# A selective scan with a LoRA feed-forward: VectorE writes the step size into the decays' buffer, and ScalarE's copies go

## The reference

```
h = layernorm(x) * (1 + ca) + sa
xp = h @ x_proj_w.T                      # 32 columns for dt, then B (16), C (16)
dt = softplus(xp[:, :32] @ dt_proj_w.T + dt_proj_b)
dA = exp(dt[..., None] * A);  dBx = dt[..., None] * B[:, None, :] * h[..., None]
state = dA_t * state + dBx_t;  y_t = sum over the 16 states of state * C_t
x = x + ga * (y + D * h)
h = layernorm(x) * (1 + cb) + sb
gate = h @ gate_w.T + (h @ gate_a.T) @ gate_b.T      # up alike, rank 16
hidden = silu(gate) * up                             # 2752 wide
x = x + gb * (hidden @ down_w.T + (hidden @ down_a.T) @ down_b.T)
```

## Time and profile before

| | |
|---|---|
| device time, median of 3 (range) | 2398.21 us (2397.32 to 2401.29) |
| profiled execution, its time | 2402.57 us |
| profiled execution, its span | 2400.6 us |
| TensorE busy | 2085.1 us (87%) |
| VectorE, ScalarE, GpSimd busy | 1446.0, 1430.1, 1545.0 us |
| the start, before pass 0 | 0 to 383 us |
| passes 0 and 1 begin | 383, 729.6 us |
| passes 2 and 3 begin | 1078.7, 1440.7 us |

### The profile page before, as it was taken

The page is one execution under the profiler, slowest core; times in us unless marked ns, Lnnn a source line. Parts: engine busy times, 40 slices in busy tenths (PEclk is TensorE's granted clock), DMA queues, the critical chain, the costliest instruction groups (busy, mean ns, idle before and its releaser), DMA issues.

```text
span 2400.6 us, 34580 instructions
## 1 busy us (share of the span) xinstructions
PE 2085.1 (87%) x11700; PEld 1888.9 (79%) x11700; DVE 1446.0 (60%) x2118; ACT 1430.1 (60%) x2798; POOL 1545.0 (64%) x960
## 2 busy tenths in 40 slices
PE   6587754877778989979999989999989999999999
PEld 3243334877767888868999978999979999999998
DVE  4665676767665688755778756678757775211111
ACT  3776766767655677665676655676656565532332
POOL 1576668988867876857876857876859897100000
PEclk9798877999889999989999999999999999999999
DMA  8777634666757677656666656666658777787785
GB/s 334 259 267 229 187 122 154 230 224 227 240 177 256 201 248 238 219 195 237 198 237 226 212 188 242 194 239 225 215 189 263 257 240 267 232 279 260 252 273 197
DMA packets 156032, 547.89 MB, mean 228 GB/s; under 512 B 17104, under 2 KB 29648, under 8 KB 152784
## 3 DMA queue, kind: packets, MB, share of 16 engines
q1 hardware_dynamic: 155856, 545.68, 68.0%
HBM read 498.32 MB, written 47.30 MB: 227 GB/s over the span
## 4 chain that ended last, share of the span: by engine, by line
PE 53%; DVE 16%; ACT 13%; issue 8%; POOL 5%; DMA 4%; SPq 0%; DVEq 0%; ACTq 0%; POOLq 0%
PE FP L762 43%; DVE ring L1168 7%; PE FP L650 4%; DVE ring L1053 3%; POOL ring L1284 2%; ACT SC L831 2%; PE FP L679 2%; ACT whi L990 2%; ACT sqb L950 2%; DVE FP L1143 1%; DMA raw<-w_gu 1%; POOL y L1257 1%; PE FP L786 1%; PE FP L624 1%; PE FP L628 1%
## 5 line engine op out<-in xcount | busy, mean ns | idle before, releaser
L1284 POOL TENSOR_TENSOR ring<-ring,c_row 128x736 f32<-128x736 f32 (+2 forms) x372 | 621.6, 1671 | 350.7 <-ACT hst L848 350.2
L762 PE MATMUL FP<-xhi,whi 128*128 128x368 f32 (+2 forms) x2160 | 713.0, 330 | 106.6 <-ACT dtb L955 27.3
L831 ACT ACTIVATE SC<-dtb,aneg 128x368 f32<-128x368 f32 (+2 forms) x768 | 409.3, 544 | 529.7 <-DVE ring L1168 525.2
L762 PE MATMUL FP<-xhi,wlo 128*128 128x368 f32 (+2 forms) x2160 | 703.7, 326 | 0.0
L762 PE MATMUL FP<-xlo,whi 128*128 128x368 f32 (+2 forms) x2160 | 703.6, 326 | 0.0
L1168 DVE TENSOR_TENSOR_SCAN ring<-SC,hst,ring 128x368 f32<-128x368 f32 (+1 forms) x640 | 579.7, 947 | 6.5 <-ACT SC L831 6.5
L1257 POOL TENSOR_TENSOR y<-y,ring 128x736 f32<-128x736 f32 (+1 forms) x320 | 555.0, 1734 | 13.7
L762 PEld LDWEIGHTS FP<-xhi,whi 128*128 128x128 f32 x2160 | 422.9, 196 | 120.7 <-ACT whi L990 66.0
L990 ACT ACTIVATE whi<-raw 128x1024 fp32r<-128x1024 f32 (+2 forms) x408 | 409.1, 1009 | 145.0 <-PE FP L786 69.7
L762 PE MATMUL FP<-hhi,whi 128*128 128x368 f32 (+5 forms) x1188 | 393.1, 331 | 66.2 <-POOL hlo L1305 46.6
L762 PEld LDWEIGHTS FP<-xlo,whi 128*128 128x128 f32 x2160 | 421.9, 195 | 1.1
(11 more groups left out here) (106 smaller groups left out, 2236.4 us busy)
## 6 DMA issues: line engine op xcount, KB each, us to landing
wlo<-lo_scratch SPq DMA_DIRECT2D x249, 576.0 KB, 4.4
raw<-w_gu SPq DMA_DIRECT2D x249, 512.0 KB, 5.0
raw<-w_dn SPq DMA_DIRECT2D x107, 448.0 KB, 4.1
wlo<-lo_scratch SPq DMA_DIRECT2D x91, 448.0 KB, 3.9
raw<-w_dn SPq DMA_DIRECT2D x53, 512.0 KB, 4.5
wlo<-lo_scratch SPq DMA_DIRECT2D x51, 512.0 KB, 4.0
raw<-w_gu SPq DMA_DIRECT2D x44, 576.0 KB, 4.7
lo_scratch<-wlo SPq DMA_DIRECT2D x44, 576.0 KB, 6.4
```

Source lines behind the costliest of these rows:

```text
L762: last = mm(out, w, x, start=(start and k == 0 and e == 0), stop=(stop and k == n - 1 and e == 2))
L831: A(decays(c, n, a), tile_of(dtb, c, i), ACT.Exp, scale=aneg[:, i * NS + s:i * NS + s + 1]).then_inc(a_da[a], 1)
L1284: G.tensor_tensor(buf, buf, over_pair(c_of(k)), ALU.mult).then_inc(g_hc, 1)
```

## The change

VectorE's sum is written to `dtb`, and not to the bank, so the copy and its semaphore go; whatever waited for the copy waits for the sum. The product L1148 then reads the sum from `dtb`. In the list the piece `keep` is gone, and a bank of a step-size tile counts as free from `soft` on.

```diff
-    for k, kind in enumerate(("dt", "sp", "soft", "keep")):
+    for k, kind in enumerate(("dt", "sp", "soft")):
         HEAD_AT.setdefault(33 + 3 * i + k, []).append((kind, i))
...
-    out += [("ini", 0, 0), ("soft", 0, 0), ("sp", 0, 1), ("keep", 0, 0), ("soft", 0, 1), ("keep", 0, 1), ("first",)]
+    out += [("ini", 0, 0), ("soft", 0, 0), ("sp", 0, 1), ("soft", 0, 1), ("first",)]
...
-        for k, kind in zip((0, 1, 3, 4), ("dt", "sp", "soft", "keep")):
+        for k, kind in zip((0, 1, 3), ("dt", "sp", "soft")):
...
-        return place[{"proj": ("xs", *item[1:]), "dt": ("keep", *item[1:]), "row": ("rowc", *item[1:]), "col": ("late", late_of(item[1]))}[kind]]
+        return place[{"proj": ("xs", *item[1:]), "dt": ("soft", *item[1:]), "row": ("rowc", *item[1:]), "col": ("late", late_of(item[1]))}[kind]]
...
             elif kind == "dt":
-                engine.wait_ge(a_keep, ND * user[1] + user[2] + 1)
+                engine.wait_ge(v_add, ND * user[1] + user[2] + 1)
...
                 elif n == 0:
-                    pe.wait_ge(a_keep, ND // PAIRS)
+                    pe.wait_ge(v_add, ND // PAIRS)
...
                 if c == 0 and s == 0:
-                    act.wait_ge(a_keep, 2 * q + 2)
+                    act.wait_ge(v_add, 2 * q + 2)
                 elif c and n == 0:
-                    act.wait_ge(a_keep, ND * (c + 1))
+                    act.wait_ge(v_add, ND * (c + 1))
...
-                elif kind == "keep":
-                    _, c, i = p
-                    t = ND * c + i
-                    act.wait_ge(v_u, t + 1)
-                    A(tile_of(dtb, c, i), bank_of("dt", c, i), ACT.Copy).then_inc(a_keep, 1)
...
-                    V.tensor_tensor(bank, bank, tile_of(dtb, c, i), ALU.add).then_inc(v_add, 1)
+                    V.tensor_tensor(tile_of(dtb, c, i), bank, tile_of(dtb, c, i), ALU.add).then_inc(v_add, 1)
                     dve.wait_ge(v_add, t + 1)
                     dve.wait_ge(a_ini, PAIRS * c + i // 2 + 1)
-                    V.scalar_tensor_tensor(out=tile_of(hb, c, i), in0=bank, scalar=modc(GA, i), in1=tile_of(hb, c, i),
+                    V.scalar_tensor_tensor(out=tile_of(hb, c, i), in0=tile_of(dtb, c, i), scalar=modc(GA, i), in1=tile_of(hb, c, i),
                                            op0=ALU.mult, op1=ALU.mult).then_inc(v_u, 1)
```

More of the change, by code:

```diff
@@ L384, in build @@
         a_xs, a_part, a_sp, a_fac = sem("xs_rounded"), sem("abs_ready"), sem("exp_ready"), sem("factor_ready")
-        a_ini, a_keep = sem("h_times_d_ready"), sem("dt_kept")
+        a_ini = sem("h_times_d_ready")
         a_da = [sem(f"decay{a}_ready") for a in range(2)]
```

## The result

The changed kernel takes 2425.69 us (median of 5; 2424.78 to 2433.28) against 2398.21 us (median of 5; 2397.32 to 2401.29): slower, the ratio is 1.0115 with a 95% interval of 1.0098 to 1.0131. The forecast was 2406, 2391 to 2417. The profiled execution of the changed kernel took 2433.28 us, 7.6 more than the median, and its span is 2431.5.

A forecast was written before the change was run, and what follows sets the result against it. It took a chain across engines to bound the start, GpSimd pass 0, and TensorE pass 2; -6.5 - 0.8 + 15.2 = +7.9 us took the profiled 2402.57 to 2410.5, or 2406 us unprofiled, range 2391 to 2417.

The forecast's parts named there:

- The product's charge: VectorE's 48 products: each is charged what is left of GpSimd's instruction at its start, less 0.2 us; 38.8 us in all.
- The waits at units 33 and 52: TensorE in passes 2 and 3: the new bank plan makes these units wait some 4 us for VectorE's sum.
- (c): VectorE's product: with two SBUF inputs it waits for GpSimd; +15.2 us on the path, bounds 0 and 38.8.
- where VectorE has slack: Passes 1 to 3: the product's block is mostly hidden there; 1.5, 0.6 and 0.6 us are charged.
- the 8 us: Start, before 383 us: share taken of the 17.6 us block, since VectorE waits 1 to 3 us in many groups.
- (b): Bank plan: banks free one piece earlier, some TensorE waits go and others come; net -0.8 us, bounds -9 and +6.
- Pass 1's gain of 3: Pass 1, shorter chunk: the new bank plan comes out at -3 us there.
- moved pieces: Plan: three pieces per pass move by one unit without the copy's weight; taken at 0, 1 us a pass either way.
- (a): ScalarE: the 48 copies go, 21.1 us of its time, mostly hidden in the passes; -6.5 us.
- The fifth: Rival on the product's block: more than 10 us over those taken are on the path; +32 us, 2430; chance 0.15.
- its two ways: The fifth: all 38.8 us are on the chain, or the product waits for more than one GpSimd instruction.
- Rival 2: TensorE: the 27.8 us of waits go and none takes their place; 2360 to 2385 us; chance 0.07.

The follow-up runs named there:

- e1: The changed kernel, but the product reads the PSUM bank, so only the two SBUF inputs are gone: 2407.08 us, ratio 1.0039 to the kernel before.
- e3: The changed kernel with the list and bank plan of before (an empty piece keep stays): 2424.81 us, ratio 1.0112 to the kernel before.
- e4: e3 with the product reading the PSUM bank, so only the 48 copies are gone from the kernel before: 2396.68 us, ratio 0.9984 to it.
- e8: e4, but chunk 3's eight products, made in pass 1, have two SBUF inputs: 2402.36 us, +0.20% over e4.
- e9: e4, but chunk 0's eight products, made in the start, have two SBUF inputs: 2396.63 us, +0.05% over e4.
- e10: e4, but chunk 1's eight products, made late in the start, have two SBUF inputs: 2405.80 us, +0.41% over e4.
- e6: e4 with the empty piece given no weight, so the order of the change with the old bank rule: 2400.19 us, -0.06% to the kernel before.

## Why the prediction was wrong, step by step

**What was right.** The change's mechanisms and the side on which it ends. The product's charge, read from GpSimd's residues under the starts in the trace of before, was 38.8 us; the changed kernel has 37.8 more, with the mean (1360 ns) and the maximum (2810) near those named. The Trainium skill's rule (page "SBUF — State Buffer", section "Who interferes with whom") agrees: with two inputs in SBUF the product waits until GpSimd's instruction is over (2.80 us in place of 0.55), and with one input it does not (in e1 all 48 take 27.5 us, as before). The waits at units 33 and 52 were put at 4 and 3.9 us and came out at 4.37 and 3.68.

**The step that failed** is the share of (c) that lies on the path, "(c) +15.2 us". By e3 against e4 it is 11.2, 6.7, 6.8, 1.8 and 1.6 us for the start and passes 0 to 3, 28.1 in all, against 8, 4.5, 1.5, 0.6 and 0.6. Passes 2 and 3 were 1.2 and 1.0 too low. Pass 1 failed most: the forecast took it together with passes 2 and 3, "where VectorE has slack", but e8 shows that its 6.1 us of block cost 6.9, about half in waits and half in TensorE's slower clock, a cost that (c) did not have. In the start the 8 us, "chosen as half, without a row that says so", were three too low, and the reason given, that VectorE waits 1 to 3 us for a broadcast, is true behind chunk 0's products alone (1.4 to 2.6 us behind four of them, none behind chunk 1's). Chunk 0's 6 us cost nothing and chunk 1's 12 cost 10 to 12 (e9, e10). These rows stood in the trace of before; I had read the idle time as a mean over the stage.

**(b) failed as well**: -0.8 forecast, against +13 without the block (e1 against e4, 0.55%). The single waits were right, but three sums were not. Pass 1's gain of 3 did not come (349.1 in e1): unit 16 starts 1.7 us sooner in the pass than in e4, and unit 20 no longer does. In passes 2 and 3 the new plan costs 6.4 and 3.6 us (e1 against e4) and not 1.1. By the unit starts of the change and of before, in pass 2 unit 33's wait leaves 1.2 us (0.75 forecast), unit 52's wait and clock cost 5.8 (5.4 forecast) and 4.0 come back by unit 58; and the first units, at which the forecast did not look, cost 2.1 up to the start of unit 3 and 3.2 up to unit 4. And one list's moved pieces, taken at 0, cost 2 us by themselves (e6). Beside the block little of this is seen (the change against e3, 1.0115 and 1.0112).

**The sum** took (b) and (c) as adding up, and they do not: 13 and 28 to 31 us apart are 31 together. So the miss can't be shared out between them in one way. With the block laid on first, as here, nearly all of it is in (c); with the plan first it is -3.8 for (a), +13 for (b) and +18 for (c), and most of the miss is in (b).

**(a) was near**: -6.5 forecast, e4 shows -3.8 (-0.7 to -7.0), and that with what the copies' waits of TensorE gave back: where unit 30 no longer waits (2.89 us), unit 33 waits 1.44 instead.

**The rivals.** The fifth had the size (2430) and the condition (over 10 us more of the block on the path): 13 more were on the old plan, 3 on the new one (e1). Of its two ways the first came true; the second, more than one GpSimd instruction per product, did not: the longest, 2810 ns, is one instruction. Rival 2 is refuted by e4: with block and plan both out of the way, the 27.8 us of waits and the copies together are worth 4 us, 7 at most.

By the timed ratios the result adds up as -0.16% for the copies, +1.28% for the block, and nothing that can be told for the plan on top, 1.12% against the measured 1.15%. This is one of the two orders above.

## What to carry to other kernels

Before an operand is moved from PSUM to SBUF on VectorE, count the inputs in SBUF and lay each start of the instruction over GpSimd's timeline of the kernel as it is: that gave the cost in busy time within 3%. Then look instruction by instruction at what of it can be paid, by the idle time in the row behind it, and not by a stage's mean: in the same stretch eight blocks cost nothing and eight others nearly everything. That row alone is not enough either. In passes 2 and 3 no product has idle time right behind it, and yet of some 4.3 us of block in each only 1.8 and 1.6 were paid. And a copy that engine A makes in its idle time, with a wait that bounds nothing, is worth little to remove (4 of 21 us); giving the product, too, to the engine that blocked gave three times that (14 us). Two costs that meet on the same path are tried together before they are added up.

## What the runs showed of the hardware

A wait of TensorE can cost more than its length: 0.9 us more at unit 48 of e8 came with a unit 1.5 us longer (granted clock 0.67 in place of 1.00). It need not: unit 33 of e4 in pass 2 took 4.45 us behind a wait of 1.44, against 4.37 for the next. A product with two inputs in SBUF lasts its own time and what is left of GpSimd's instruction at its start, less 0.2 us, to within 0.01 us in all 48 of the change, up to 2.81 us. And the engine that holds is held too: 35 of the change's products end over GpSimd's next instruction, and each of those takes 0.14 to 0.32 us more than the median of its kind (1.51 us in place of 1.28 at 251.99); in the kernel before, 11 products end over one, and none of those takes over 0.03 more.
